# Attention on one core: chunks, rotation, high and low parts, column sums and normalising stand in other rounds of a step

## The reference

```python
q = queries @ Wq
kv = queries @ Wkv
k, v = jnp.split(kv, 2, axis=-1)
...
q, k = (_rope(q), _rope(k))
sim = jnp.einsum('bhid,bhjd->bhij', q, k) * SCALE
attn = jax.nn.softmax(sim, axis=-1)
out = jnp.einsum('bhij,bhjd->bhid', attn, v)
out = out.transpose(0, 2, 1, 3).reshape(b, n, HEADS * DIM_HEAD)
return out @ Wout + bout
```

## Time and profile before

| | |
|---|---|
| median of 3 runs | 2106.55 us (2104.82 to 2110.93) |
| profiled execution, its time | 2106.52 us |
| its span in the profile | 2104.7 us |
| TensorE busy over the span | 1888.7 us, 90% |
| VectorE | 1602.6 us, 76% |
| GpSimd | 1493.7 us, 71% |
| ScalarE | 841.3 us, 40% |

### The profile page before, as it was taken

How to read it: one execution, slowest core, us unless ns; L and a number is a source line. 1 busy time by engine, 2 the same in 40 slices (tenths; PEclk the granted TensorE clock), 3 DMA queues, 4 the chain that set the end, 5 groups by cost and what they waited for, 6 DMA issues and landing times. The chain is left out here.

```text
span 2104.7 us, 29315 instructions
## 1 busy us (share of the span) xinstructions
PE 1888.7 (90%) x10916; PEld 1172.3 (56%) x10916; DVE 1602.6 (76%) x1968; ACT 841.3 (40%) x1101; POOL 1493.7 (71%) x699
## 2 busy tenths in 40 slices
PE   5957888865999999999999999999999999999499
PEld 4746878863554555545555555455555555554289
DVE  5457999956888887888888888888878888885164
ACT  4632223211444444444444444444444444444232
POOL 0115565521888888888888888888888888888543
PEclk9988989986999999999999999999999999999799
DMA  8830000030111112111111211111221111111286
GB/s 303 326 133 6 16 13 16 16 106 22 29 49 46 46 42 85 52 57 46 42 46 51 77 57 51 47 43 45 61 76 57 46 41 46 41 36 42 89 283 220
DMA packets 141561, 152.84 MB, mean 73 GB/s; under 512 B 41840, under 2 KB 97776, under 8 KB 141168
## 3 DMA queue, kind: packets, MB, share of 16 engines
q1 hardware_dynamic: 141424, 151.03, 22.4%
HBM read 95.95 MB, written 55.05 MB: 72 GB/s over the span
## 5 line engine op out<-in xcount | busy, mean ns | idle before, releaser
L1120 POOL TENSOR_TENSOR acc<-acc,prob 128x1024 f32<-128x1024 f32 x384 | 948.4, 2470 | 131.2 <-ACT prob L1155 93.9
L997 DVE TENSOR_REDUCE half_max<-m_ps 128x2 f32<-128x1024 f32 x512 | 624.7, 1220 | 257.5 <-PE m_ps L889 257.5
L1155 ACT ACTIVATE prob<-s_ps 128x1024 f32<-128x1024 f32 x512 | 497.4, 1023 | 539.1 <-PE s_ps L913 536.9
L928 PE MATMUL o_ps<-prob,v 128*64 128x512 f32 x2048 | 492.5, 602 | 0.0
L889 PE MATMUL m_ps<-k_hi,q_hi 64*128 64x512 f32 x1024 | 235.7, 456 | 68.4 <-DVE half_max L997 64.1
L928 PEld LDWEIGHTS o_ps<-prob,v 128*64 128x64 f32 x2048 | 129.9, 136 | 247.8 <-issue 191.4
L1102 POOL TENSOR_TENSOR turned<-straight,shuffled 128x512 f32<-128x512 f32 x128 | 176.1, 1376 | 120.5 <-DVE shuffled L1029 117.0
L958 PE MATMUL misc_ps<-xT,wqk 128*128 128x512 f32 x768 | 221.6, 426 | 16.8 <-DMA xT<-xn_scratch 9.7
L958 PEld LDWEIGHTS misc_ps<-xT,wqk 128*128 128x128 f32 x768 | 140.4, 196 | 142.7 <-issue 108.7
L889 PEld LDWEIGHTS m_ps<-k_hi,q_hi 64*128 64x128 f32 x1024 | 96.8, 185 | 210.2 <-DVE half_max L997 152.6
L910 PE MATMUL s_ps<-q_hi,k_hi 64*128 64x512 f32 x1024 | 203.1, 392 | 0.0
(11 more groups left out here) (129 smaller groups left out, 2417.6 us busy)
## 6 DMA issues: line engine op xcount, KB each, us to landing
v_scratch<-v_out SPq DMA_DIRECT2D x32, 512.0 KB, 2.9
wqk<-wp_scratch SPq DMA_DIRECT2D x32, 512.0 KB, 3.4
v<-v_scratch SPq DMA_DIRECT2D x32, 512.0 KB, 4.7
inv_rows<-inv_scratch SPq DMA_DIRECT2D x128, 128.0 KB, 3.1
o_scratch<-o_norm SPq DMA_DIRECT2D x64, 256.0 KB, 2.0
o_in<-o_scratch SPq DMA_DIRECT2D x8, 2048.0 KB, 10.8
xn_scratch<-p_xT SPq DMA_DIRECT2D x32, 256.0 KB, 3.6
xT<-xn_scratch SPq DMA_DIRECT2D x8, 1024.0 KB, 5.6
```

The lines of the kernel that those rows point to most:

```text
L928: ins = nc.tensor.matmul(o_ps[head * DH:(head + 1) * DH, :], v[s % 2][:, kt, at:at + DH], prob[n % SLOTS][:, head, :], start=kt == 0, stop ...
L997: nc.vector.tensor_reduce(half_max[:, half % 2, :, t % GRP, part], m_ps[:, :, :], axis=AX.X, op=ALU.max, negate=True).then_inc(half_maxed, 1)
L1120: nc.gpsimd.tensor_tensor(acc[b][:, :, :], first, prob[n % SLOTS][:, :, :], ALU.add).then_inc(added, 1)
L1155: nc.scalar.activation(prob[n % SLOTS][:, :, :], s_ps[n % 2][:, :, :], ACT.Exp).then_inc(exp_done, 1)
```

## The change

In rounds counted within a step, it moves these:

- TensorE: `project` goes from the end of rounds 1, 3, 5, 7 to right behind the second `guess` of the same round, ahead of `values`. `column_sums` goes from rounds 1 and 5 to rounds 2 and 6. `misc_table()` follows.
- VectorE: `rotate` of a chunk goes from between the two reductions of the next round to behind the second reduction of the chunk's own round. `low` goes to rounds 4, 6, 0 and 2 (K0, K1, Q0, Q1), from 3, 5, 7 and 1. `invert` goes from rounds 3 and 7 to 4 and 0, `normalise` of the even half from round 1 to round 2; that of the odd half stays in round 6.
- ScalarE: `copy_sums` goes from rounds 1 and 5 to 2 and 6. `high` stays where it was.
- GpSimd and SyncE: unchanged.

```diff
@@ misc_table
-            if r == 1 and 0 <= s - 1 < STEPS:
+            if r == 2 and 0 <= s - 1 < STEPS:
                 job("sum", s - 1, 1)
-            if r == 5 and 0 <= s < STEPS:
+            if r == 6 and 0 <= s < STEPS:
                 job("sum", s, 0)
+            if r in CHUNK_ROUND and 0 <= s + 2 < STEPS:
+                job("chunk", s + 2, CHUNK_ROUND[r])
...
-            if r in CHUNK_ROUND and 0 <= s + 2 < STEPS:
-                job("chunk", s + 2, CHUNK_ROUND[r])
@@ tensor
                         guess(s + 1, 2 * r + 1)
-                    if r == 1 and scoring(s - 1):
+                    if r in CHUNK_ROUND and scoring(s + 2):
+                        project(s + 2, CHUNK_ROUND[r])
+                    if r == 2 and scoring(s - 1):
                         column_sums(s - 1, 1)
-                    if r == 5 and scoring(s):
+                    if r == 6 and scoring(s):
                         column_sums(s, 0)
...
-                    if r in CHUNK_ROUND and scoring(s + 2):
-                        project(s + 2, CHUNK_ROUND[r])
@@ vector
-                    if r == 0 and scoring(s + 1):
-                        rotate(s + 1, Q1)
-                    if r - 1 in CHUNK_ROUND and scoring(s + 2):
-                        rotate(s + 2, CHUNK_ROUND[r - 1])
                     if scoring(s + 1):
                         maximum(s + 1, 2 * r + 1)
                         if r in (3, 7):
                             combine(s + 1, r // 4)
-                    if r == 1 and scoring(s + 1):
-                        low(s + 1, Q1)
-                    if r - 2 in CHUNK_ROUND and scoring(s + 2):
-                        low(s + 2, CHUNK_ROUND[r - 2])
-                    if r == 3 and scoring(s - 1):
+                    if r in CHUNK_ROUND and scoring(s + 2):
+                        rotate(s + 2, CHUNK_ROUND[r])
+                    if r in (0, 2) and scoring(s + 1):
+                        low(s + 1, Q0 if r == 0 else Q1)
+                    if r in (4, 6) and scoring(s + 2):
+                        low(s + 2, K0 if r == 4 else K1)
+                    if r == 4 and scoring(s - 1):
                         invert(2 * (s - 1) + 1)
-                    if r == 7 and scoring(s):
-                        invert(2 * s)
-                    if r == 1 and scoring(s - 1):
+                    if r == 0 and scoring(s - 1):
+                        invert(2 * (s - 1))
+                    if r == 2 and scoring(s - 1):
                         normalise(2 * (s - 1))
                     if r == 6 and scoring(s - 1):
                         normalise(2 * (s - 1) + 1)
```

More of the change, by code:

```diff
@@ L1176, in _ @@
                         high(s + 1, Q1)
-                    if r - 2 in CHUNK_ROUND and scoring(s + 2):
+                    if r in (3, 5, 7) and scoring(s + 2):
                         high(s + 2, CHUNK_ROUND[r - 2])
```

## The result

The changed kernel takes 2175.3 us (median of 4, 2173.25 to 2176.74) against 2107.6 for the kernel before on the same chip: a ratio of 1.032, 95% interval 1.030 to 1.034. It is 3% slower. The profiled execution took 2173.97 us with a span of 2172.2.

A forecast was written before the change was run, and what follows sets the result against it. TensorE, 97% busy, was taken as the bound, its `guess` matmuls waiting for `half_max`. A step of 43.86 + 2 x (1.02 + 1.11) = 48.12 against 45.66, over 29 steps, less 1, gave 2106.5 + 70 = 2177 us, range 2106 to 2196.

The forecast's parts named there:

- The work of a step is unchanged and `rotate` hides: All rounds: work stays 43.86 us a step; `rotate` ends 0.3 us before the next reduction could start, old losses (1.80) go.
- Rounds 2 and 6: `low`, then the rotated sum, then `normalise`, 1.02 us lost in round 3: VectorE is blocked by GpSimd's addition, then its rotated sum; `guess` comes late, 1.02 us lost in rounds 3 and 7 each.
- Rounds 0 and 4: the addition is 0.26 us ahead of `low`: `low` asks 0.26 us too late and waits for GpSimd's addition; next reduction at 6.40, `guess` late by 0.80 us.
- `spread_rows` adds to it through `project`: Rounds 1 and 5: `project` waits for `spread_rows` and starts at 8.4; loss 1.1 us per half step.
- The end of a blocking: VectorE gets in 0.14 us before the GpSimd addition's recorded end; blocking for the whole instruction would give 2201.
- Small things taken as nothing: Sums, reciprocals and DMAs cost nothing; a missed landing would cost up to 3.1 us a step.
- `turn_max` of 0.40: TensorE, round 0: `guess` 0.40 us behind `turn_max`, as in the kernel before, within a round of 4.78 us.
- The signs: What the profile after would show, among it TensorE's busy share at some 92% and GpSimd's at 83%.
- its own case: `low` and `normalise` blocked in both halves of the step, 2177 us, own range 2162 to 2195; chance 0.50.
- Rival B: Only rounds 2 and 6 lose, as `low` gets in before the addition in rounds 0 and 4: 2114 us; chance 0.14.
- Rival D: One half of the step is blocked, the other not: a step of 47.01 us, 2146 us; chance 0.13.
- Rival C: `normalise` goes right behind `low`, before GpSimd's next operation, and nothing is lost: 2054 us, faster; chance 0.15.

The follow-up runs named there:

- Experiment 2: Changed kernel with `low` of rounds 0 and 4 put between the two reductions; 2109.5 us, 1.002 of the kernel before.
- Experiment 5: Changed kernel with a GpSimd fill of a spare tile ahead of the addition in rounds 0 and 4: 512 columns 2112.1 us, 32 columns 2176.8 us.
- Experiment 3: Changed kernel with GpSimd's additions of tiles replaced by a fill of the same tile, so no column sums; 2038.0 us, one execution.
- experiment 1: Changed kernel with `low` of rounds 2 and 6 put between the two reductions; 2046.5 us, 0.972 of the kernel before.
- experiment 4: Kernel before with only TensorE's and ScalarE's part of the change, VectorE's order as before; 2166.6 us, 1.029.
- experiment 6: Kernel of experiment 4 with `column_sums` moved behind `values`; 2110.4 us, 1.002 of the kernel before.
- experiment 7: Kernel before with only VectorE's part of the change, TensorE and ScalarE as before; 2336.0 us, one execution.

## Why the prediction was right

It said 2177 and the kernel takes 2175.3. The steps, each against its row:

- *The work of a step is unchanged and `rotate` hides.* Right, but for `turn_max` (last point): rounds 2 and 6 take 5.23 and 5.25 (5.23 forecast), and the waits behind `rotate` are gone.
- *Rounds 2 and 6: `low`, then the rotated sum, then `normalise`, 1.02 us lost in round 3.* The next reduction came at T2 + 7.11 (7.07 forecast), `guess` at 8.38 (8.34); the round lasted 7.03, 1.07 lost. `low` 1.73, `normalise` 1.78. Experiment 2 leaves this loss alone standing.
- *Rounds 0 and 4: the addition is 0.26 us ahead of `low`.* It was 0.27. The reduction came at T0 + 6.44 (6.40), round 1 lasted 7.09 (7.07). Experiment 5 shows that the margin was the cause: 0.12 us more work on GpSimd leaves it ahead and changes nothing, 0.52 puts it behind and the loss goes.
- *`spread_rows` adds to it through `project`.* `project` began at T0 + 8.26 (8.4).
- *The end of a blocking.* By the rule "for the whole instruction" of the Trainium skill ("SBUF — State Buffer", "Who interferes with whom"; the section says it of VectorE's 2-port modes, and the prediction took it over for two SBUF inputs) the estimate was 2201; the rows gave 2177. The trace sides with the rows on the size: the addition of 1018.06 has its recorded end at 1020.43, and `low` ends at 1020.98, which is 0.69 behind 1020.29. It sides with the page on what matters: a VectorE instruction with two SBUF inputs blocks, and "issue order, not op shape, decides who blocks". Experiment 3 agrees with its other half too: a fill, which only writes, blocks nothing (0.68). Whether the ports come free before the addition ends, or its record runs on behind its end, no run here tells.
- *Small things taken as nothing*: the DMAs of the sums never held up `normalise` between 600 and 1900 us.
- *The one term that was off* is the `turn_max` of 0.40, really 0.26: round 0 lasts 4.63, not 4.78. In the forecast this more than offset the two losses, which were 0.05 and 0.02 larger, so a step takes 47.97 and not 48.12. It is 0.30 a step too much, some 9 us, against 0.14 too little, 4 us. With `turn_max` alone put right the forecast would have been 2168, so part of the closeness of 2177 to 2175.3 is luck.
- *The signs.* TensorE's busy share fell to 94% (92 forecast) and GpSimd's to 84 (83).

The larger luck is in the margin. The order of the two engines in rounds 0 and 4 hung on 0.26 us, a sum of ten terms by the prediction's own count, and the prediction gave its own case a chance of 0.50. The terms held, and the margin came out at 0.27; nothing before the run could say so.

Rival B (only rounds 2 and 6 lose) lost on the margin of 0.26 us. The large fill of experiment 5 makes its very condition true, GpSimd later in rounds 0 and 4, and takes 2112.1; experiment 2 reaches the same loss by another edit and takes 2109.5. B's price was 2114. Rival D (one half of the step blocked, the other not) is out, since both halves show the same rounds. Rival C lost because the rotated sum got in between `low` and `normalise`. No run makes its condition true: in experiment 1 `normalise` is still blocked (1.72). That kernel only has C's outcome, nothing lost, and takes 2046.5 where C's price was 2054.

## What to carry to other kernels

Where VectorE and GpSimd both read two operands from SBUF, the duration of a VectorE instruction in a profile is a property of its place as much as of the instruction: 0.68 to 2.9 us for the same one here. Before moving such an instruction, write down for the new place what GpSimd will be doing at the moment of asking and how long the next wait on VectorE can be put off; a place where GpSimd waits for another engine was free (0.68 in experiment 1), and a move of one `low` decided some 6% of the kernel. A layout that spreads the work evenly over the rounds is not better in itself. Here it took away the round of 6.82 us in which TensorE had enough work of its own while VectorE stood blocked.

## What the runs showed of the hardware

- A VectorE instruction with two operands in SBUF (128x512) gets in about 0.14 us before the recorded end of GpSimd's addition, and the two engines alternate when both have work waiting (1.73, 1.74 and 1.78 in a row in the changed kernel). The one that asks 0.10 us earlier wins (experiment 5). A fill of 0.95 us on GpSimd, which only writes, held up nothing (experiment 3).
- TensorE's granted clock fell to 0.50 for some 3 us after waits of 1.30 and 0.70 with one `guess` between, in 18 of 29 steps by the steps' lengths, and cost some 1.6 us each time (experiment 4). It did not fall after one of 1.30 alone (experiment 6), and it did after one of 2.81 (experiment 7). What exactly decides it was not tried.
